# An early-fusion transformer block: the second pair's embedding moved into the prologue, and the negative maxima split on GpSimd

## The chip, the core and the metric

The kernel runs on one core of one Trainium2 chip. Its engines are TensorE (PE, with its weight loads PEld), VectorE (DVE), ScalarE (ACT), GpSimd (POOL) and SyncE (SP), each with its own instruction stream; they wait for each other on semaphores. The metric is the device time of one execution, in microseconds (us), as the median of several runs.

## The reference

Eight images go through one block, and everything is float32.

```python
def tokenise(x, W):                       # x: 8, C=64, T=128, V=64
    xp = pad(x, 8 steps of T at the end, mode='edge')
    patches = xp[:, :, idx, :]            # 16 patches of 16 steps, stride 8
    xf = rfft(patches, axis=steps, norm='ortho')      # 9 frequencies
    return concat([xf.real, xf.imag]) @ W.T           # 1024 tokens of 64
h = concat([tokenise(x, W), txt])         # 1056 tokens: 1024 + 32 of text
h = h + attention(layernorm(h))           # 4 heads of 16, softmax, projection
h = h + moe(layernorm(h))                 # 8 experts 64-128-64, gelu, top 2 of 8
```

## The kernel before

**Pairs and slots.** Two images make a pair, one on partitions 0 to 63 and one on 64 to 127; there are four pairs. The patches, the transform and the weight are folded into one matrix `tok_m`, so that a half of a pair's tokens (512) is embedded by eight *steps* accumulating in one PSUM bank; a step is two float32 matmuls, one for each image, which the trace shows as four passes (`embed`, L1205). Then follow centring, variances (L458), the inverse roots by Newton steps on VectorE (`newton_step`, L479), their spreading by matmul (L505) and the scaling to `xn` (L1105). The attention takes the eight images one after the other in eight *slots* (`run_phase1`, L364). A slot has three chunks of queries (384, 384, 288) of 33 *units* each: a unit computes scores for one head and one tile of 128 keys (L1196, bf16), ScalarE exponentiates them (L932), and eight units later, each fourth unit, four heads are multiplied with the values (L1174, float32). Three banks hold scores. The last part of the kernel, the experts, is not touched.

**Maxima.** The softmax subtracts each query's exact maximum. So the scores are also computed beforehand with queries on the partitions (`maxima`, L1217; a matmul of 512 columns, L1233) and reduced by VectorE out of three further banks (L1044): 73 entries a slot with the shifts, hosted some 41 units ahead, most of an image's first chunk beside the previous image. After a chunk's last maximum VectorE takes the negative maximum (`negm`, L1058), splits it in three bf16 parts by four small dependent operations (L1067 to L1074), TensorE transposes them (*shift*, L1255), VectorE copies the result (`m_part`, L1083) and SyncE stores it under the query stack by three DMAs (L795); the first scores of the chunk (L1192) wait for these. `max_order` (L74) writes the order out: the shift of a chunk stands behind the first two maxima of the next chunk.

**Queries and keys.** A projection (L1287) is split in three bf16 parts by ScalarE, VectorE and GpSimd (L941, L1089, L1092, L861), and DMAs interleave the parts into the stacks `qs` and `ks` (L752; for the first image ScalarE issues those of `ks`, L948). The first maxima wait for the stacks.

**What goes on beside the units** is set by lists of unit numbers at the head of the file (`AT_EMBED`, `AT_TOKENISE`, `AT_FINISH` and so on) and put in one order for all engines by `side_steps` (L305): each engine walks the same list and does its own part, in order. Slot 0 tokenises pair 1, slot 2 pair 2, slot 4 pair 3; its 16 embedding steps stand at every second unit, 34 to 48 and 50 to 64. Slots 2, 4 and 6 also finish a pair's attention (L1313), for which GpSimd normalises the heads (L867). All of these take turns in one PSUM bank, counted by `side_full` and `side_free`.

**The prologue** does the same for pair 0 without cover: x in eight transfers and edges, embedding, normalisation, projection, stacks, values (L1292, evacuated by ScalarE, L954 and L961), and then the 32 maxima and shifts that belong before slot 0. SyncE loads x of pair 1 behind the stacks, 14 of 21 transfers at once (`X_EARLY`) and the others beside slot 0 (`load_x`, L673). `xt` is one buffer of 17 blocks, so a pair can be loaded only when the one before it is embedded; a half reads its own eight blocks and the one after them.

The order of an image's maxima is written out like this:

```python
order += [(0, c, 0), (0, c, 1), (0, c - 1, None)] + [(0, c, i) for i in range(2, MAX_OF[c])]
```

## Time and profile before

| what | value |
|---|---|
| median of 3 runs | 852.92 us (852.79 to 853.16) |
| the profiled execution's own time | 856.51 us |
| its span, first to last instruction | 854.7 us |
| TensorE busy | 783.5 us, 92% of the span |
| VectorE busy | 542.5 us, 63% |
| ScalarE busy | 460.8 us, 54% |
| GpSimd busy | 131.6 us, 15% |
| mean granted clock of TensorE | 0.945 |
| slot 0 begins, slot 1 begins | 89.8 us, 182.3 us |

The profile is one execution. A matmul's end is modelled, so that a busy TensorE isn't necessarily at its peak. The granted clock is given as a share of 2.4 GHz: 1.00 is that level, 0.50 the other, 1.2 GHz. In a row of the timeline or of a group, `out<-in` names the tiles, `x4` the number of instructions, and what stands in brackets is the idle time before them and what ended it. The chain of waits is followed back from the last instruction, at each step to what released it.

### The profile page before, as it was taken

The numbers are of one execution on the slowest core, as the hardware profiler recorded it, in microseconds if no ns is written. First come the engines' busy times: TensorE is split into PE (matmuls) and PEld (weight loads), VectorE is DVE, ScalarE is ACT, GpSimd is POOL, SyncE is SP. The second block draws the span as 40 slices with busy tenths as digits, with TensorE's granted clock in tenths as the row PEclk, the third lists the DMA queues.
The fourth block names the chain that finished last, engine by engine and source line by source line (L and its number), as shares of the span: only waits on it lengthen the run. The fifth ranks groups of instructions, "written<-read, shape, count | busy, mean of one in ns | idle before, by whom it ended". The sixth has DMA issues, their size and how long they took to land.

```text
span 854.7 us, 14341 instructions
## 1 busy us (share of the span) xinstructions
PE 783.5 (92%) x5352; PEld 304.7 (36%) x5352; DVE 542.5 (63%) x1181; ACT 460.8 (54%) x1069; POOL 131.6 (15%) x148
## 2 busy tenths in 40 slices
PE   1858899999999999999998999999988899999995
PEld 1342222433342243334224333433334344545442
DVE  5037664688876468887646588778864174656642
ACT  1100454566674456667445466766755655564662
POOL 0010100012000001201000110010100055463664
PEclk9955699999999999999999699999999999999998
DMA  9319121016621001662100110120000736465571
GB/s 194 76 52 196 58 59 38 2 48 143 112 79 66 1 2 58 133 112 86 59 2 1 41 53 2 48 97 1 15 2 2 140 81 133 101 133 100 118 140 26
DMA packets 61933, 60.03 MB, mean 70 GB/s; under 512 B 23840, under 2 KB 54056, under 8 KB 61864
## 3 DMA queue, kind: packets, MB, share of 16 engines
q1 hardware_dynamic: 59264, 57.58, 30.7%
q10 hardware_dynamic: 2599, 1.54, 0.9%
q8 instruction: 42, 0.69, 0.3%
q14 instruction: 28, 0.22, 0.1%
HBM read 38.88 MB, written 2.57 MB: 48 GB/s over the span
## 4 chain that ended last, share of the span: by engine, by line
PE 75%; DVE 14%; ACT 3%; DMA 3%; issue 2%; SPq 1%; POOL 0%; ACTq 0%; POOLq 0%; DVEq 0%
PE bank L1174 14%; PE bank L1196 13%; PE bank L1233 11%; PE bank L1210 8%; PE bank L1345 6%; PE bank L1328 6%; DVE max_parts L1044 5%; PE bank L1287 3%; PE bank L1179 2%; PE bank L462 2%; PE bank L513 2%; DMA q_stack<-m_part 1%; PE bank L638 1%; DMA proj_in<-in_L_attn_w_proj 1%; ACT probs L932 1%
## 5 line engine op out<-in xcount | busy, mean ns | idle before, releaser
L1044 DVE TENSOR_REDUCE max_parts<-bank 128x1 f32<-128x512 f32 x512 | 329.4, 683 | 123.4 <-PE bank L1233 121.9
L932 ACT ACTIVATE probs<-bank 128x384 f32<-128x384 f32 (+1 forms) x768 | 311.0, 466 | 175.8 <-PE bank L1196 174.1
L1196 PE MATMUL bank<-q_stack,k_stack 99*128 99x384 bf16 (+1 forms) x768 | 225.6, 322 | 2.7 <-ACT probs L932 2.4
L1233 PE MATMUL bank<-k_stack,q_stack 96*128 96x512 bf16 x512 | 205.2, 404 | 4.4 <-DVE max_tail L1052 1.8
L1174 PE MATMUL bank<-probs,v_tiles 128*32 128x384 f32 (+1 forms) x1536 | 156.4, 480 | 2.2 <-ACT heads_out L917 2.1
L1196 PEld LDWEIGHTS bank<-q_stack,k_stack 99*128 99x128 bf16 x768 | 72.0, 99 | 189.3 <-ACT probs L932 139.6
L984 ACT ACTIVATE hid<-bank,biases 128x704 f32<-128x704 f32 x96 | 77.7, 844 | 57.9 <-PE bank L1345 57.6
L1131 DVE SCALAR_TENSOR_TENSOR prod<-bank,biases,cwb 128x352 f32<-128x352 f32 x96 | 55.3, 580 | 64.6 <-PE bank L1328 54.8
L881 POOL TENSOR_TENSOR acc<-acc,prod 128x352 f32<-128x352 f32 x84 | 78.2, 931 | 59.7 <-DVE prod L1131 55.7
L861 POOL TENSOR_TENSOR part<-qk_rest,part 128x352 bf16<-128x352 f32 x24 | 20.4, 850 | 361.6 <-DVE part L1092 361.6
L1233 PEld LDWEIGHTS bank<-k_stack,q_stack 96*128 96x128 bf16 x512 | 50.6, 99 | 54.9 <-DVE max_parts L1044 30.3
L1328 PE MATMUL bank<-hid,w_sb 128*64 128x352 f32 x384 | 68.9, 478 | 1.3 <-DVE prod L1131 1.3
L1210 PE MATMUL bank<-x,tok_m 128*64 128x512 f32 x256 | 68.2, 631 | 1.7 <-DVE tok_m L1026 1.1
L867 POOL TENSOR_TENSOR on<-heads_out,recip 128x352 f32<-128x352 f32 x24 | 21.9, 934 | 218.3 <-DMA recip<-recip_rows 218.3
L1174 PEld LDWEIGHTS bank<-probs,v_tiles 128*32 128x32 f32 x1536 | 30.8, 109 | 61.1 <-ACT probs L932 40.6
L1345 PE MATMUL bank<-xn,w_sb 64*128 64x352 f32 x192 | 35.6, 488 | 0.6 <-ACT hid L984 0.6
L1328 PEld LDWEIGHTS bank<-hid,w_sb 128*64 128x64 f32 x384 | 23.4, 137 | 34.8 <-issue 27.9
L1345 PE MATMUL bank<-xn_odd,w_sb 64*128 64x352 f32 x192 | 35.2, 483 | 0.6 <-ACT hid L984 0.6
L941 ACT ACTIVATE part<-bank 128x352 bf16<-128x352 f32 x24 | 11.1, 463 | 33.7 <-PE bank L1287 33.5
L925 ACT ACTIVATE probs_tail<-bank 128x384 f32<-128x384 f32 (+1 forms) x24 | 11.1, 462 | 33.7 <-PE bank L1192 33.7
L513 PE MATMUL bank<-ident_half,root_part 128*64 128x128 bf16 (+1 forms) x432 | 18.1, 231 | 10.4 <-DVE root_part L503 7.4
L1287 PE MATMUL bank<-xn,qkT 64*128 64x352 f32 x48 | 26.0, 637 | 1.0 <-DVE xn L1105 0.6
(146 smaller groups left out, 541.9 us busy)
## 6 DMA issues: line engine op xcount, KB each, us to landing
cwb<-gates_by_expert SPq DMA_DIRECT2D x24, 704.0 KB, 11.3
x<-in_x SPq DMA_DIRECT2D x48, 256.0 KB, 6.9
q_stack<-part SPq DMA_DIRECT2D x48, 132.0 KB, 2.4
k_stack<-part SPq DMA_DIRECT2D x42, 132.0 KB, 2.5
x<-in_x SPq DMA_DIRECT2D x4, 576.0 KB, 11.3
h_res<-h_new SPq DMA_DIRECT2D x4, 528.0 KB, 3.0
recip<-recip_rows SPq DMA_DIRECT2D x32, 66.0 KB, 2.5
h_all<-h_res SPq DMA_DIRECT2D x4, 528.0 KB, 3.0
```

What stands on the lines that cost most here:

```text
L881: nc.gpsimd.tensor_tensor(dst, h2_all[:, p, chunk[c]] if e == 0 else dst, prod[:, n % N_PROD, :], ALU.add).then_inc(summed, 1)
L932: nc.scalar.activation(probs[:, group % 3, h, 0:n], src, ACT.Exp, scale=SCALE).then_inc(exp_done, 1)
L984: nc.scalar.activation(hid[:, n % N_HID, :, :], psum[:, first:first + 2, 0:CH], ACT.Gelu, bias=b1_sb[:, e:e + 1]).then_inc(gelu_done, 1)
L1044: nc.vector.tensor_reduce(max_parts[:, c, H * j + h, i % 2:i % 2 + 1], src[:, :], AX.X, ALU.max)\
L1131: nc.vector.scalar_tensor_tensor(out=prod[:, n % N_PROD, :], in0=banks[4 + n % 2][:, 0:CH], scalar=b2_sb[:, e:e + 1], in1=cwb[p % 2][:, e, ...
L1174: last = nc.tensor.matmul(o_bank[32 * h:32 * h + 32, 0:n], v_tiles[par][:, kt, h, :], probs[:, group % 3, h, 0:n], start=(kt == 0), stop=F ...
L1196: last = nc.tensor.matmul(bank[:, 0:n], ks[par][0:ROWS + 3, h, P * kt:P * kt + P], qs[par][0:ROWS + 3, h, QC[qc]], start=True, stop=True)
L1210: last = nc.tensor.matmul(bank[D * bp:D * bp + D, :], tok_m[:, part, :], xt[bp][:, first:first + NPATCH // 2, t4, :], start=(part == 0), s ...
L1233: last = nc.tensor.matmul(bank[:, :], queries(h, j), ks[par][0:ROWS, h, HALF * (i % 2):HALF * (i % 2) + HALF], start=True, stop=True)
L1287: last = nc.tensor.matmul(bank[:, 0:CH], qkT[rows, :], xn[rows, chunk[i]], start=True, stop=True)
L1328: last = nc.tensor.matmul(banks[4 + n % 2][D * bp:D * bp + D, 0:CH], w2_sb[:, m % E, :], hid[:, n % N_HID, bp, :], start=True, stop=True)
L1345: last = nc.tensor.matmul(banks[2 * (n % 2) + bp][:, 0:CH], w1_sb[rows, e, :], xn2[p % 2][rows, chunk[c]], start=True, stop=True)
```

## The change

**Loading.** The second pair's x is loaded in halves by eight larger transfers and four edges: the first half when pair 0's first half is embedded, the second when its second half is, both issued by SyncE ahead of the copy of `h_res`; the text follows that. `X_EARLY` and slot 0's loads are gone. **Embedding.** The sixteen steps of pair 1 and the two evacuations into `h_new` leave slot 0: six steps come behind the values of image 0, ten among the prologue's maxima (`AHEAD_BESIDE`: behind entries 3, 6, 9, ... of the 32). Slot 0 keeps the rest of the tokenising (`settle`). In slots 2 and 4 the steps stand in pairs, two at each fourth unit. **Values.** Image 0's are evacuated by VectorE. **Negative maxima.** The four splitting operations go from VectorE to GpSimd, for all 24 chunks, and the shift comes behind three maxima of the next chunk rather than two. The diff, cut to its core:

```diff
@@ -59,7 +59,7 @@
...
 AT_STACK = [1, 3]
-AT_EMBED = [list(range(34, 49, 2)), list(range(50, 65, 2))]
+AT_EMBED = [[34, 34, 38, 38, 42, 42, 46, 46], [50, 50, 54, 54, 58, 58, 62, 62]]
@@ -67,15 +67,19 @@
...
 X_DMAS = 4 * (X_CUTS + 1) + 1
-X_EARLY = 14
-AT_LOAD = {"first": [2 + 3 * k for k in range(X_DMAS - X_EARLY)], "load": [30 + 3 * k for k in range(X_DMAS)]}
+X_SECOND = 13
+AT_LOAD = [30 + 3 * k for k in range(X_DMAS)]
+AHEAD = 2
+AHEAD_BEFORE, AHEAD_BESIDE = 6, [3, 6, 9, 12, 15, 18, 21, 24, 29, 30]
...
+SHIFT_AFTER = 3
...
-    order = [(0, 0, 0), (0, 0, 1), (-1, NCH - 1, None)] + [(0, 0, i) for i in range(2, MAX_OF[0])]
+    order = [(0, 0, i) for i in range(SHIFT_AFTER)] + [(-1, NCH - 1, None)] + [(0, 0, i) for i in range(SHIFT_AFTER, MAX_OF[0])]
     for c in range(1, NCH):
-        order += [(0, c, 0), (0, c, 1), (0, c - 1, None)] + [(0, c, i) for i in range(2, MAX_OF[c])]
+        order += [(0, c, i) for i in range(SHIFT_AFTER)] + [(0, c - 1, None)] + [(0, c, i) for i in range(SHIFT_AFTER, MAX_OF[c])]
@@ -210,6 +214,7 @@
...
         neg_max = sem("neg_max")
+        neg_found = sem("neg_found")
@@ -284,8 +289,9 @@
...
         g_values0 = USES["tokenise"] + USES["project"]
-        g_slot0 = g_values0 + USES["values"]
-        g_slot1 = g_slot0 + 2 * USES["project"] + USES["tokenise"]
+        g_ahead = g_values0 + USES["values"]
+        g_slot0 = g_ahead + AHEAD
+        g_slot1 = g_slot0 + 2 * USES["project"] + USES["tokenise"] - AHEAD
@@ -316,10 +322,8 @@
...
                 order.append(("normalise", AT_NORMALISE.index(u), b - 1, 1 - par, q, g))
-            if "load" in stages and u in AT_LOAD["load"]:
-                order.append(("load", AT_LOAD["load"].index(u), None, None, q + 2, g))
-            if "first" in stages and u in AT_LOAD["first"]:
-                order.append(("load", X_EARLY + AT_LOAD["first"].index(u), None, None, 1, g))
+            if "load" in stages and u in AT_LOAD:
+                order.append(("load", AT_LOAD.index(u), None, None, q + 2, g))
@@ -327,18 +331,22 @@
...
                     ("tokenise", "tokenise", AT_TOKENISE, None, None, q + 2),
+                    ("settle", "tokenise", AT_TOKENISE, None, None, q + 2),
...
                 if name in stages:
+                    done = AHEAD if name == "settle" else 0
+                    g = g - done
+                    if name == "tokenise":
+                        for i in range(2):
+                            for part, at_part in enumerate(AT_EMBED[i][:-1]):
+                                if u == at_part:
+                                    order.append(("embed", (i, part), None, None, pair, g))
...
                         order.append(("vary", AT_VARY.index(u), None, None, pair, g))
-                    if u in at:
+                    if u in at and at.index(u) >= done:
                         order.append((stage, at.index(u), t, tpar, pair, g))
-                    if stage == "tokenise":
-                        for i in range(2):
-                            if u in AT_EMBED[i][:-1]:
-                                order.append(("embed", (i, AT_EMBED[i].index(u)), None, None, pair, g))
-                        if u in AT_ROOT:
-                            order.append(("root", 1 + AT_ROOT.index(u), None, None, pair, g))
+                    if stage == "tokenise" and u in AT_ROOT:
+                        order.append(("root", 1 + AT_ROOT.index(u), None, None, pair, g))
@@ -357,7 +365,7 @@
         NEXT = ("following", "normalise")
-        BESIDE = {0: ("following", "first", "tokenise", "project"), "odd": NEXT + ("load", "project"),
+        BESIDE = {0: ("following", "first", "settle", "project"), "odd": NEXT + ("load", "project"),
@@ -391,9 +399,15 @@
...
                 side("values", i, 0, None, 0, g_values0)
-            for u in range(MAX_PLACE[0], 0):
-                for _, c, i, n in hosted(u, True, False):
-                    side("maxima" if i is not None else "shift", (c, i, n), 0, 0, None, None)
+            ahead = [("embed" if part < 7 else "tokenise", (half, part) if part < 7 else half, None, None, 1, g_ahead)
+                     for half in range(AHEAD) for part in range(8)]
+            for step in ahead[:AHEAD_BEFORE]:
+                side(*step)
+            early = [found for u in range(MAX_PLACE[0], 0) for found in hosted(u, True, False)]
+            for k, (_, c, i, n) in enumerate(early):
+                side("maxima" if i is not None else "shift", (c, i, n), 0, 0, None, None)
+                if k in AHEAD_BESIDE:
+                    side(*ahead[AHEAD_BEFORE + AHEAD_BESIDE.index(k)])
@@ -442,8 +456,8 @@
...
             if isinstance(t, int) and t == 0:
-                at = n if n < 2 else n - 1
-                return at, n % 3, at - 1 if n in (3, 4) else at - 2
+                at = n if n < SHIFT_AFTER else n - 1
+                return at, n % 3, at - 1 if n in (SHIFT_AFTER + 1, SHIFT_AFTER + 2) else at - 2
@@ -688,19 +702,22 @@
...
-        def load_first_x(eng):
...
-            for half, (first, n) in enumerate(((0, NPATCH // 2 + 1), (NPATCH // 2 + 1, NPATCH // 2 - 1))):
+        def load_half_x(eng, pair, half, blocks, done):
...
+            first, n = blocks
+            for bp in range(2):
+                for th in range(2):
+                    eng.dma_start(xt[bp][C * th:C * th + C, first:first + n, :, :],
+                                  x[2 * pair + bp].rearrange("c (j h t) v -> h c j t v", h=2, t=4)[th, :, first:first + n])\
+                       .then_inc(done, 16)
+            if half == 1:
...
                     for th in range(2):
-                        eng.dma_start(xt[bp][C * th:C * th + C, first:first + n, :, :],
-                                      x[bp].rearrange("c (j h t) v -> h c j t v", h=2, t=4)[th, :, first:first + n])\
-                           .then_inc(x_half[half], 16)
-            for bp in range(2):
-                for th in range(2):
-                    eng.dma_start(xt[bp][C * th:C * th + C, NPATCH, :, :],
-                                  x[bp][:, T - 1:T, :].broadcast_to([C, 4, V])).then_inc(x_half[1], 16)
-            eng.dma_start(text_in[:, :, :], txt[0:2].rearrange("b t d -> t b d")).then_inc(x_half[1], 16)
+                        eng.dma_start(xt[bp][C * th:C * th + C, NPATCH, :, :],
+                                      x[2 * pair + bp][:, T - 1:T, :].broadcast_to([C, 4, V])).then_inc(done, 16)
...
+        def load_text(eng, pair, done):
+            eng.dma_start(text_in[:, :, :], txt[2 * pair:2 * pair + 2].rearrange("b t d -> t b d")).then_inc(done, 16)
@@ -743,7 +760,9 @@
...
             def _(sp):
-                load_first_x(sp)
+                load_half_x(sp, 0, 0, (0, NPATCH // 2 + 1), x_half[0])
+                load_half_x(sp, 0, 1, (NPATCH // 2 + 1, NPATCH // 2 - 1), x_half[1])
+                load_text(sp, 0, x_half[1])
@@ -781,10 +800,6 @@
...
                         stack_parts(t, par, range(3, 6))
-                        if isinstance(t, int) and t == 0:
-                            sp.wait_ge(side_full, 3)
-                            for k in range(X_EARLY):
-                                load_x(sp, 1, k)
@@ -800,9 +815,14 @@
...
                         load_ffn(sp)
-                    elif stage == "tokenise" and isinstance(pair, int) and pair == 0 and i == 3:
+                    elif stage == "tokenise" and pair == 0 and i < 2:
...
+                        sp.wait_ge(side_full, i + 1)
+                        load_half_x(sp, 1, i, (NPATCH // 2 * i, NPATCH // 2), x_loaded)
+                    elif stage == "tokenise" and pair == 0 and i == 3:
...
                         sp.dma_start(h_res[:, :], h_new[:, :]).then_inc(h_copied, 16)
+                        load_text(sp, 1, x_loaded)
@@ -860,6 +880,21 @@
...
                                                 ALU.subtract).then_inc(part3_done, 1)
+                    elif stage == "maxima" and i[1] == MAX_OF[i[0]] - 1:
...
+                        c = i[0]
+                        k = NCH * t + c
+                        kinds = slice(0, 1) if c < NCH - 1 else slice(1, 3)
+                        pool.wait_ge(neg_found, k + 1)
+                        nc.gpsimd.tensor_copy(neg_part[:, kinds, :, 0, :], negm[:, kinds, :, :]).then_inc(neg_step, 1)
+                        pool.wait_ge(neg_step, 3 * k + 1)
+                        nc.gpsimd.tensor_tensor(neg_rest[:, kinds, :, :], negm[:, kinds, :, :],
+                                                neg_part[:, kinds, :, 0, :], ALU.subtract).then_inc(neg_step, 1)
+                        pool.wait_ge(neg_step, 3 * k + 2)
+                        nc.gpsimd.tensor_copy(neg_part[:, kinds, :, 1, :], neg_rest[:, kinds, :, :]).then_inc(neg_step, 1)
+                        pool.wait_ge(neg_step, 3 * k + 3)
+                        nc.gpsimd.tensor_tensor(neg_part[:, kinds, :, 2, :], neg_rest[:, kinds, :, :],
+                                                neg_part[:, kinds, :, 1, :], ALU.subtract).then_inc(neg_max, 1)
@@ -946,7 +981,7 @@
...
                             act.dma_start(ks[par][n:ROWS:len(PARTS), :, 0:L], qk_part[k][D:P, :]).then_inc(stacked, 16)
-                    elif stage == "values":
+                    elif stage == "values" and t > 0:
@@ -1053,7 +1088,6 @@
...
                             dve.wait_ge(max_done, at + 1)
-                            step = 4 * (NCH * t + c)
@@ -1062,17 +1096,7 @@
...
                                                                    AX.X, ALU.max, negate=True)
-                            last.then_inc(neg_step, 1)
-                            dve.wait_ge(neg_step, step + 1)
-                            nc.vector.tensor_copy(neg_part[:, kinds, :, 0, :], negm[:, kinds, :, :]).then_inc(neg_step, 1)
-                            dve.wait_ge(neg_step, step + 2)
-                            nc.vector.tensor_tensor(neg_rest[:, kinds, :, :], negm[:, kinds, :, :],
-                                                    neg_part[:, kinds, :, 0, :], ALU.subtract).then_inc(neg_step, 1)
-                            dve.wait_ge(neg_step, step + 3)
-                            nc.vector.tensor_copy(neg_part[:, kinds, :, 1, :], neg_rest[:, kinds, :, :]).then_inc(neg_step, 1)
-                            dve.wait_ge(neg_step, step + 4)
-                            nc.vector.tensor_tensor(neg_part[:, kinds, :, 2, :], neg_rest[:, kinds, :, :],
-                                                    neg_part[:, kinds, :, 1, :], ALU.subtract).then_inc(neg_max, 1)
+                            last.then_inc(neg_found, 1)
@@ -1090,6 +1114,21 @@
...
                         nc.vector.tensor_copy(qk_part[1][:, chunk[i]], qk_rest[:, chunk[i]]).then_inc(part2_done, 1)
+                    elif stage == "values" and t == 0:
+                        bank = full(dve, i, g)
+                        if i < 2:
+                            tiles = slice(KT // 2 * i, KT // 2 * i + KT // 2)
+                            for bp in range(2):
+                                last = nc.vector.tensor_copy(
+                                    v_tiles[bp][:, tiles, :, 0:DH],
+                                    bank[:, :].rearrange("p (k a h d) -> p a k h d", a=2, h=H, d=DH)[:, bp])
+                        else:
+                            for h in range(H):
+                                rows = slice(32 * h, 32 * h + 32)
+                                for bp in range(2):
+                                    last = nc.vector.tensor_copy(v_tail[bp][rows, 32 * h:32 * h + DH],
+                                                                 bank[rows, DH * bp:DH * bp + DH])
+                        last.then_inc(side_free, 1)
@@ -1268,7 +1307,7 @@
...
                             elif half == 0:
-                                pe.wait_ge(x_loaded, 16 * X_DMAS * pair)
+                                pe.wait_ge(x_loaded, 16 * (X_SECOND + X_DMAS * (pair - 1)))
...
```

## Rows read from the trace of the kernel before

**Rows 1.** the page: the span and the granted clock in 40 slices (tenths)

```profile
span 854.7 us, 14341 instructions
...
PEclk9955699999999999999999699999999999999998
```

**Rows 2.** stretches, slots 0, 1, 2, 4: busy per engine, clock, DMA share, GB/s

```profile
89.76:182.34 92.58, 90.55 (x575) 30.16 (x575) 57.78 (x125) 47.62 (x115) 4.86 (x6) 0.91 0.13 36
...
182.34:242.59 60.25, 58.35 (x425) 20.12 (x425) 49.65 (x99) 41.28 (x105) 5.50 (x7) 1.00 0.52 108
...
242.59:330.99 88.40, 86.74 (x607) 30.80 (x607) 57.11 (x123) 48.27 (x125) 5.03 (x6) 0.98 0.10 35
...
390.83:484.82 93.99, 91.14 (x606) 32.05 (x606) 57.22 (x123) 48.35 (x125) 5.26 (x6) 0.93 0.10 33
```

**Rows 3.** the chain that ended last, prologue: start us, us, what

```profile
62.13 5.83 DMA k_stack<-part
...
87.93 1.79 DMA q_stack<-m_part
...
89.76 0.51 PE bank L1192 x4
```

**Rows 4.** stretches of the prologue and of the start of slot 0

```profile
0.00:22.00 22.00, 3.51 (x44) 2.94 (x44) 12.92 (x25) 2.18 (x6) 0.20 (x4) 1.00 1.05 194
...
68.00:89.80 21.80, 17.86 (x47) 3.50 (x47) 19.65 (x37) 0.07 (x2) 0.00 (x0) 0.50 0.89 154
...
89.80:102.50 12.70, 12.70 (x36) 3.75 (x37) 7.60 (x14) 5.61 (x12) 2.55 (x3) 0.52 0.09 28
```

**Rows 5.** timeline of TensorE, first pair's embedding: windows from 20 and from 27.69

```profile
22.33 16.25 PE L1210 MATMUL bank<-x,tok_m 128*64 128x512 f32 x64 [1.12 <-DVE tok_m L1026]
...
27.69 10.89 PE L1210 MATMUL bank<-x,tok_m 128*64 128x512 f32 x50
```

**Rows 6.** timeline, values in the prologue and a VectorE copy in slot 0

```profile
57.11 2.07 PE L1292 MATMUL bank<-vT,xn 128*128 128x128 f32 x8 [1.11 <-DVE qk_rest L1089]
...
63.13 0.66 ACT L954 ACTIVATE v_tiles<-bank 128x256 f32<-128x256 f32 x2 [6.63 <-issue]
...
67.07 1.00 ACT L961 ACTIVATE v_tail<-bank 32x16 f32<-32x16 f32 x8 [0.46 <-PE bank L1296]
...
152.57 0.69 DVE L1096 COPY h_new<-bank 128x512 f32<-128x512 f32 x1
```

**Rows 7.** DMA issues of x: KB each, median us to landing

```profile
x<-in_x SPq DMA_DIRECT2D x48, 256.0 KB, 6.9
```

**Rows 8.** the chain that ended last, slot 0

```profile
105.45 0.33 PE bank L1196 x2
...
117.64 1.01 PE bank L1210 x4
...
121.93 0.27 PE bank L1196
```

**Rows 9.** timeline of SyncE, the early transfers of x

```profile
63.09 12.86 SPq L679 DMA_DIRECT2D x<-in_x  x14
```

**Rows 10.** groups of instructions on GpSimd: busy, mean ns, idle before

```profile
L861 POOL TENSOR_TENSOR part<-qk_rest,part 128x352 bf16<-128x352 f32 x24 | 20.4, 850 | 361.6 <-DVE part L1092 361.6
...
L1412 POOL MEMSET const-float32-1.0<- 128x1 f32 x1 | 0.1, 98 | 0.0
```

**Rows 11.** the chain that ended last, slot 1's second chunk

```profile
197.17 1.27 DVE max_parts L1044 x2
...
200.26 1.78 DMA q_stack<-m_part
```

**Rows 12.** a stretch of slot 4

```profile
464.00:470.00 6.00, 4.11 (x69) 2.29 (x67) 5.47 (x19) 2.21 (x7) 0.00 (x0) 1.00 0.00 0
```

**Rows 13.** the chain that ended last, slot 4

```profile
467.72 0.18 DVE neg_part L1067
...
468.49 0.48 DVE xn L1105
```

## The prediction

> **What bounds the kernel now.** I read the page first, for the span and the clock row [rows 1]: TensorE is granted its upper level (2.4 GHz) nearly everywhere, and the lower one (1.2 GHz) in two places, slices 3 and 4 (43 to 85 us, from the table of stretches on to 102) and one slice near 480. Then I cut the attention into its slots [rows 2]. TensorE is busy 90.6 of 92.6 us in slot 0, 86.7 of 88.4 in slot 2 and 58.4 of 60.3 in slot 1, so work taken from it there shortens the slot; slots 0, 2 and 4 are longer than the odd ones because a pair is tokenised beside them. Last, the chain of waits of the prologue [rows 3]: the stacks land at 68.0 (62.13 + 5.83), first maxima run to the shift whose DMA starts at 87.93, and slot 0 begins at 89.76. In these 21.8 us VectorE is busy 19.7, 0.61 us for each of some 31 maxima, TensorE at the lower clock 17.9; in the first 12.7 us of slot 0 TensorE is busy throughout, still at 0.52 of its clock [rows 4].
>
> The profiled execution took 856.5 us (span 854.7 and 1.8 around it), 3.6 above the median of 852.9. I work out a difference within the profile and take it from the median.
>
> **A. The 16 embedding steps of pair 1, before slot 0.** What precedes them: values 0 leaves TensorE at 59.2 [rows 6]; in the kernel before, ScalarE issues six stack DMAs first and evacuates only at 63.13. On VectorE, which is idle there, each half of the values is two 256-column copies; from the 512-column copy of 0.69 us [rows 6] I take 0.75 for both (ScalarE: 0.66). The eight small copies were 1.00 on ScalarE; I take 1.1. Then: 59.2 + 0.75 + 2.07 + 0.75 + 0.34 + 1.1 = 64.3 us, from which embedding may start (0.3 estimated for the tail's small matmuls).
>
> Is x there? A pair is 16 transfers of 256 KB [rows 7] and four edge rows a quarter of that, 4.35 MB. Half of it may be issued when the first half of pair 0 is embedded (31.7 by the slow and fast passes below), the rest at 38.6 when the second is (the end of the 16.25 us row, [rows 5]). At the 194 GB/s of the first 22 us [rows 4] that is 11 us each, so all lands near 54; at the 154 of the maxima stretch, near 60. SyncE now issues fourteen in 12.86 us, 0.92 each [rows 8]; the second eight keep it until 46, with the copy of h_res and the text behind them, and it is free again before the stacks. The copy of h_res so lands some 7 us later; its reader is the second pair's first evacuation, beyond 70. Cost nothing, and if x were late by t, t.
>
> Six steps (24 matmul passes) come ahead of the maxima. In pair 0's embedding 50 passes took 10.89 us, 0.218 each, 0.87 a step; the whole 64 took 16.25 [rows 5], which fits 12 passes at twice that. So I take 12 slow passes and 12 fast: 5.2 + 2.6 = 7.8, ending at 72.1. The ends: 5.2 if the clock is up already (69.5), 10.5 if it doesn't rise (74.8). First maxima at 68.0 become 72.1: **+4.1** (+1.5 to +6.8). The stacks can only land earlier, x no longer sharing their queue, and hide behind the six steps.
>
> Ten steps lie among the maxima. At the upper clock an isolated step is 1.01 us and the score matmul after it 0.27 where a pair takes 0.33, so 0.105 more [rows 9]: 1.11 us. With three maxima at 0.22 (512 columns, as a pass of the embedding) that is 1.77 against VectorE's 1.83. They fit, barely, with two finished banks in hand; the last two lie behind the shift, where TensorE waits for its DMA. Their evacuation (0.69) is VectorE's and also behind the shift. I take **+0.3**.
>
> **B. Slot 0.** It loses 16 isolated steps: 16 x 1.11 = **-17.8**. And it starts at the upper clock: of 12.6 slow us TensorE would need 6.3, but VectorE's 7.6 [rows 4] and gaps of 0.8 then bound, so 8.4: **-4.2**. The sum, 70.6, stands against slot 1's 60.3 [rows 2] with some 10 to 12 us of the remaining tokenising and second projection on top, so no floor is broken. The slower end, clock down again at the slot's start, is 0 in place of -4.2.
>
> **C. Steps in pairs, slots 2 and 4.** The second step of a pair is free of the switch: 1.11 - 0.87 = 0.24, eight times a slot, two slots: **-3.9**. A block of 1.9 us lets ScalarE run dry, but over slot 2 it is busy 0.49 of each unit's 0.89 [rows 2]; if it does hurt, the other end is +2.
>
> **D. Negative maxima on GpSimd, the shift one maximum later.** VectorE loses four operations a chunk, in slot 4 0.77 us from the first (467.72) to the next tile's work (468.49) [rows 13]. GpSimd shows none so small: above, 0.85 us for 352 columns; below, 0.10 for a one-column memset [rows 10]. By the line between them 12 columns are 0.13; with semaphores I take 0.22, four are 0.9, near the lower row because the operand is. For two-input elementwise work the Trainium skill (GPSIMD Engine Reference, 4.1 Engine selection) calls GpSimd the wrong engine, about twice slower than VectorE; with the 0.18 of such an operation now doubled for two or all of the four, the chain would be 1.1 to 1.4. No run here shows it yet.
>
> Three maxima (1.83 us) now cover this chain instead of two, and VectorE reaches the shift's copy no later: the two maxima at 197.17 start 0.8 after they could [rows 11]. So slots 1, 3, 5 and 7, whose second chunk waits for the shift's DMA (until 202.04 in slot 1 [rows 11]), gain 0.8 each, **-3.2**. The 19 other hand-overs cost nothing of themselves, hidden by scores and maxima. In slots 0, 2 and 4 the chain of roots and maxima holds TensorE (busy 4.1 of 6.0 us, [rows 12]) and the four operations stand right in it [rows 13]: 3 x 0.77 = **-2.3**. GpSimd's normalising now queues behind the split; in slot 6 the finishing matmul, a unit after the shift, then waits, an estimated **+0.6**, and slot 7's last shift, with no maxima to cover it, **+0.3**.
>
> **Sum**: 4.1 + 0.3 - 17.8 - 4.2 - 3.9 - 3.2 - 2.3 + 0.9 = -26.1; 852.9 - 26.1 = **826.8 us**.
>
> **Rivals.**
> **The clock stays down through the prologue.** For it: TensorE was fully busy for 12.7 us at the lower level before it rose [rows 4]. Against: by its passes, the first embedding rose within its first 5 us [rows 5], and this is the same work. Six steps then end at 74.8 (+6.8); a group of three maxima and a step costs 3 x 0.43 + 1.9 = 3.2 against 1.83, eight times (+11), the last two +2; no clock is won back in slot 0. With C and D (-8.5): 19.8 - 17.8 - 8.5 = -6.5: 846.4. The Trainium skill (TensorE: Matmul & The Clock Gate, Part 1) has the lower level as the default that activity lifts; the embedding row agrees, the start of slot 0 less plainly. 10%.
> **GpSimd is dear (the slower case).** At 0.85 an operation the chain is 3.4 us, the copy of the shift 1.8 later than now, and TensorE stands in order before the shift with scores queued behind it. With 24 hand-overs, all exposed, +43; the 14 outside the prologue and the tokenising slots alone, +25. Against A to C's -21.5 that is 856 to 875, say 864. With all exposed it decides from about 0.62 us an operation (24 x (1.8 - 4 x 0.23) = 21). For it: only the 0.85 row has this engine's arithmetic. Against: 352 columns aren't 12. 4%.
> **The change moves the work but gains nothing**: x late by 20 us or more, or the ten steps starve VectorE. Against: the 10 us in hand above. Near 852. 2%.
> **Clock dips.** The slice near 480 is a dip behind that starved stretch; slot 4 is 5.6 longer than slot 2 for it [rows 2]. With D the stretch is fuller and the dip may go: 821.2, 20%. Or it comes at slot 0's start as well: 831.0, 15%. Both lie in the range.
>
> **Numbers.** Forecast as it stands, 49%. The range, 815.5 to 839, holds it, both dips, and the ends of A to D short of the low-clock prologue. A measurement can tell 0.2% (1.7 us) from no change. Faster 0.94: all but the dear GpSimd, the empty case and a remainder; slower 0.04, same 0.02.
>
> **What would show it.** In the changed profile: x landed before 60; 24 embedding passes between 64 and 72, then maxima at 0.61 us spacing; full granted clock by 72 and at slot 0's start, near 94.2; slot 0 near 70 long; slots 2 and 4 shorter by 2 to 3; GpSimd's four operations about 0.2 us each, no wait of the shift matmul for them over 0.5. It is wrong if the maxima run slower than 0.7 us apart, if slot 0 starts after 98, or if the shift matmuls wait for GpSimd by a microsecond each.

## The result and the profile after

| | before | changed |
|---|---|---|
| median of 4 runs | 853.04 us | 832.83 us |
| range | 852.79 to 854.58 | 832.56 to 835.82 |
| profiled execution, its span | 856.51, 854.7 | 832.62, 830.8 |
| mean granted clock in it | 0.945 | 0.966 |

The change is faster: the ratio is 0.9742, with a 95% interval of 0.9688 to 0.9795; 20.2 us less, where 26.1 less were forecast (826.8; the range was 815.5 to 839). The page of the changed kernel, its span and its clock row, against [rows 1]:

```profile
span 830.8 us, 14333 instructions
...
PEclk9968899999999999999999999999999999999998
```

A part of slices 3 and 4 is still at the lower level (44.5 to 51.3 and 54.7 to 68.3 us), a part of slice 5 is at it too, and the dip near 480 us isn't there. By slots (slots 0, 1, 2 and 4 of the changed kernel, columns as in [rows 2]):

```profile
93.08:167.57 74.49, 72.18 (x510) 27.88 (x510) 54.40 (x112) 45.61 (x114) 7.38 (x18) 0.91 0.12 34
167.57:226.91 59.34, 57.89 (x425) 20.12 (x424) 47.41 (x87) 41.09 (x105) 7.99 (x19) 1.00 0.53 110
226.91:314.47 87.56, 84.99 (x606) 32.09 (x606) 55.13 (x111) 47.49 (x125) 7.50 (x18) 0.98 0.11 36
373.81:461.34 87.53, 84.95 (x606) 32.10 (x606) 55.14 (x111) 47.50 (x125) 7.49 (x18) 0.98 0.11 36
```

Slot 0 begins 3.3 us later and is 74.5 us long in place of 92.6; slot 1 is 0.9 shorter, slot 2 0.8. Slot 4 is 6.5 shorter, of which 5.6 are the dip that the profiled execution of before happened to have there: it had been that much longer than slot 2, at the same work. From slot 7 on nothing changed (249.0 to the end, 248.9 before). Over the two profiles that makes -23.9, without the dip -18.3; the medians say -20.2. The profiled execution of before was 3.5 above its median, so the truth lies between the two sums.

The prologue, from the timeline of the changed kernel (start us, duration, engine, line; in brackets the idle time before and what ended it), against [rows 3], [rows 5] and [rows 6]:

```profile
41.53 7.09 SPq L716 DMA_DIRECT2D x<-in_x  x4
...
57.68 0.75 DVE L1122 COPY v_tiles<-bank 128x256 f32<-128x256 f32 x2 [1.47 <-PE bank L1331]
...
61.81 1.07 DVE L1129 COPY v_tail<-bank 32x16 f32<-32x16 f32 x8 [0.46 <-PE bank L1335]
63.02 7.99 PE L1249 MATMUL bank<-x,tok_m 128*64 128x512 f32 x24 [1.28 <-DVE v_tail L1129]
70.95 0.82 PE L1272 MATMUL bank<-k_stack,q_stack 96*128 96x512 bf16 x3
...
93.08 0.35 PE L1231 MATMUL bank<-q_stack,k_stack 99*32 99x384 bf16 x4 [1.07 <-DMA q_stack<-m_part]
```

VectorE's evacuations are 0.75 and 1.07, forecast 0.75 and 1.1; the 24 passes ahead of the maxima take 7.99, forecast 7.8; the first maxima come at 71.0, forecast 72.1, and slot 0 starts at 93.1, forecast 94.2. The 1.1 us is TensorE's projection, which met a higher clock. SyncE issued x and its edges until 48.6, forecast 46, and the first stack transfer at 57.25 was not delayed; the embedding waited for VectorE's evacuation and not for x. What the forecast did not take as its case is seen a little further on, in stretches of 2 us (columns as in [rows 4]):

```profile
88.00:90.00 2.00, 1.19 (x6) 0.39 (x6) 2.00 (x5) 0.00 (x0) 0.52 (x3) 1.00 0.00 0
90.00:92.00 2.00, 2.00 (x8) 0.39 (x6) 1.09 (x3) 0.00 (x0) 0.00 (x0) 1.00 0.01 3
92.00:94.00 2.00, 0.93 (x7) 0.49 (x7) 1.24 (x3) 0.49 (x1) 0.00 (x0) 1.00 0.01 2
94.00:96.00 2.00, 1.76 (x7) 0.66 (x6) 1.38 (x4) 1.23 (x3) 0.00 (x0) 0.91 0.00 0
96.00:98.00 2.00, 2.00 (x5) 0.58 (x5) 1.45 (x3) 0.77 (x2) 0.85 (x1) 0.50 0.00 0
98.00:100.00 2.00, 2.00 (x5) 0.50 (x2) 1.79 (x4) 0.64 (x2) 0.85 (x1) 0.50 0.00 0
100.00:102.00 2.00, 2.00 (x7) 0.75 (x7) 1.17 (x3) 1.50 (x4) 0.22 (x1) 0.50 0.00 0
102.00:104.00 2.00, 2.00 (x11) 0.34 (x9) 1.61 (x3) 0.79 (x2) 0.63 (x1) 0.50 0.05 15
104.00:106.00 2.00, 2.00 (x9) 0.74 (x6) 0.69 (x1) 0.90 (x3) 0.00 (x0) 0.53 0.65 209
```

TensorE is at 2.4 GHz from 68 us through the maxima, idle for about 0.8 us before the shift and 1.07 us for the shift's DMA, and at 95.7 it falls to the lower level and stays there till 105.9 (the last row's 0.53). Slot 0's first chunk takes 26.15 us, little less than the 26.83 of before.

### The profile page after: what moved, and what is told of

Read it like the earlier page. It is cut to its first block, busy times and chain, and to the rows that moved or that the text cites. A ratio compares the mean times of both kernels' runs of the same rounds, so it can differ in the third digit from the quotient of the medians.

```text
span 830.8 us, 14333 instructions
## 1 busy us (share of the span) xinstructions
PE 762.5 (92%) x5352; PEld 306.7 (37%) x5352; DVE 529.5 (64%) x1097; ACT 455.2 (55%) x1057; POOL 151.7 (18%) x244
## 4 chain that ended last, share of the span: by engine, by line
PE 78%; DVE 10%; ACT 4%; issue 2%; DMA 2%; POOL 1%; ACTq 1%; SPq 1%; POOLq 0%; DVEq 0%
PE bank L1213 16%; PE bank L1235 14%; PE bank L1272 12%; PE bank L1249 7%; PE bank L1367 6%; PE bank L1384 6%; DVE max_parts L1079 3%; PE bank L1326 2%; PE bank L1218 2%; PE bank L527 2%; PE bank L476 2%; DVE max_tail L1087 1%; DMA q_stack<-m_part 1%; ACT probs L967 1%; PE bank L1331 1%
## 5 line engine op out<-in xcount | busy, mean ns | idle before, releaser
L967 ACT ACTIVATE probs<-bank 128x384 f32<-128x384 f32 (+1 forms) x768 | 307.5, 466 | 155.6 <-PE bank L1235 154.1
L1272 PE MATMUL bank<-k_stack,q_stack 96*128 96x512 bf16 x512 | 196.3, 389 | 4.7 <-DVE max_tail L1087 3.2
L889 POOL CAST neg_part<-negm 128x12 bf16<-128x12 f32 (+1 forms) x24 | 4.7, 198 | 428.7 <-DVE negm L1092 330.2
L1249 PE MATMUL bank<-x,tok_m 128*64 128x512 f32 x256 | 66.5, 649 | 3.0 <-DVE v_tail L1129 1.3
L1249 PEld LDWEIGHTS bank<-x,tok_m 128*64 128x64 f32 x256 | 17.5, 147 | 35.5 <-issue 34.0
L1004 ACT ACTIVATE h_new<-bank 128x512 f32<-128x512 f32 (+1 forms) x8 | 3.2, 397 | 44.1 <-PE bank L1249 37.5
```

What stands on the lines that cost most here:

```text
L967: nc.scalar.activation(probs[:, group % 3, h, 0:n], src, ACT.Exp, scale=SCALE).then_inc(exp_done, 1)
L1249: last = nc.tensor.matmul(bank[D * bp:D * bp + D, :], tok_m[:, part, :], xt[bp][:, first:first + NPATCH // 2, t4, :], start=(part == 0), s ...
L1272: last = nc.tensor.matmul(bank[:, :], queries(h, j), ks[par][0:ROWS, h, HALF * (i % 2):HALF * (i % 2) + HALF], start=True, stop=True)
```

## The experiments

Because the clock falls at other places in other executions, I compare mostly the lengths of chunks, from one chunk's first scores (`L1192` in the kernel before) to the next's; where the clock is up and GpSimd splits the maxima they repeat within 0.1 us, and where VectorE splits them they differ by up to 0.4 (22.00 and 22.36 in slots 2 and 4 of `e5_early_only`). The changed kernel, e1 to e4, e5 to e8 and e9 to e12 are four groups, each measured beside the kernel before, whose median was 853.0, 857.1, 859.0 and 855.6: ratios are to be compared, not medians across groups. The start of slot 0 also moves with the clock in the prologue: three kernels with the same prologue (changed, e1, e6) have it between 92.86 and 94.42. "Slot 2" gives its three chunks; "odd" is slot 3's first chunk.

| kernel | median (range) us | ratio, 95% interval | slot 0 starts | its first chunk | slot 0 | odd | slot 2 |
|---|---|---|---|---|---|---|---|
| before | 853.0 | 1 | 89.76 | 26.83 | 92.58 | 19.34 | 21.99, 38.23, 28.18 |
| changed | 832.8 (832.6 to 835.8) | 0.974 (0.969 to 0.980) | 93.08 | 26.15 | 74.49 | 19.11 | 22.34, 37.37, 27.85 |
| e1_singles | 835.9 (830.7 to 838.4) | 0.974 (0.969 to 0.979) | 92.86 | 26.06 | 74.43 | 19.15 | 22.34, 38.34, 27.41 |
| e2_split_vector | 839.4 (833.3 to 840.4) | 0.977 (0.972 to 0.982) | 92.76 | 22.62 | 71.38 | 19.83 | 21.77, 37.37, 28.39 |
| e3_fill | 830.3 (829.4 to 831.2) | 0.968 (0.964 to 0.972) | 91.69 | 21.82 | 70.15 | 19.12 | 22.33, 37.38, 27.84 |
| e4_shift_two | 831.3 (831.2 to 835.4) | 0.970 (0.966 to 0.974) | 92.69 | 21.42 | 69.80 | 18.77 | 22.33, 37.48, 27.78 |
| e5_early_only | 842.1 (835.3 to 844.2) | 0.980 (0.974 to 0.985) | 92.95 | 21.85 | 70.67 | 19.23 | 21.99, 38.23, 28.18 |
| e6_pairs_moved | 830.2 (828.0 to 834.2) | 0.967 (0.962 to 0.972) | 94.42 | 26.16 | 74.51 | 19.13 | 22.34, 36.41, 27.43 |
| e7_values_scalar | 836.6 (831.7 to 839.8) | 0.975 (0.969 to 0.981) | 97.19 | 26.03 | 74.40 | 19.13 | 22.33, 37.38, 27.81 |
| e8_best | 825.6 (824.8 to 826.3) | 0.962 (0.958 to 0.966) | 90.10 | 21.82 | 70.17 | 19.12 | 22.33, 36.41, 27.42 |
| e9_no_fill | 829.2 (825.2 to 832.0) | 0.969 (0.964 to 0.973) | 89.85 | 21.81 | 69.76 | 19.10 | 22.34, 36.40, 27.81 |
| e10_fill_last | 826.5 (825.5 to 827.1) | 0.966 (0.962 to 0.970) | 89.50 | 21.81 | 70.39 | 19.12 | 22.34, 36.41, 27.84 |
| e11_normalise_first | 822.6 (820.5 to 828.9) | 0.962 (0.958 to 0.967) | 90.39 | 21.82 | 70.19 | 19.12 | 21.57, 36.41, 27.42 |
| e12_four_ahead | 822.5 (821.4 to 824.1) | 0.961 (0.957 to 0.966) | 89.77 | 21.81 | 69.76 | 19.13 | 21.57, 36.41, 28.04 |

### The early embedding alone

```diff
 (the changed kernel, with the split on VectorE, SHIFT_AFTER = 2 and single steps)
-AT_EMBED = [[34, 34, 38, 38, 42, 42, 46, 46], [50, 50, 54, 54, 58, 58, 62, 62]]
+AT_EMBED = [list(range(34, 49, 2)), list(range(50, 65, 2))]
-SHIFT_AFTER = 3
+SHIFT_AFTER = 2
```

> The kernel before with the early loading, the early embedding and the values on VectorE alone: the split is on VectorE, the shift behind two maxima, the steps of slots 2 and 4 single. The forecast's A and B: slot 0 starts at 94.2 and is 70.6 long, 835 in all; with its clock dip at the start 839. My theory after the first runs: slot 0 starts near 93 and is 71 to 75 long with the clock, slots 2 and 4 88.4, odd slots 59.8 to 60.2 as in the kernel before; 837 to 840, so that the split and the pairs together are worth 5 to 7 of the 20. Rival: the early embedding gives everything, 833.

Measured: ratio 0.980, so about four fifths of the gain, though the intervals of the two ratios overlap. In its profiled execution slot 0 starts at 92.95 and is 70.67 long, all but 3.4 us at the upper clock (forecast 94.2 and 70.6); slot 2 is that of before, slot 4 is 89.1 long. Both slots as stretches of that profile:

```profile
92.95:163.62 70.67, 68.01 (x512) 26.65 (x512) 55.88 (x125) 45.02 (x114) 4.87 (x6) 0.98 0.12 36
224.39:312.79 88.40, 85.34 (x605) 30.31 (x605) 57.17 (x123) 48.27 (x125) 5.01 (x6) 1.00 0.11 35
```

The median is over my 837 to 840, and its six executions lie in two groups, 835.3 and 835.4 with a mean clock of 0.973 and four from 840.7 to 844.2 with 0.957 to 0.960. The four are 5 to 9 us longer at their lower mean clock; where in them it fell isn't recorded. The 70.67 agrees with the forecast partly by luck. The first chunk, which holds no embedding step, went from 26.83 to 21.85, so the clock was worth 5.0 rather than 4.2; the second chunk, which held all sixteen steps, went from 37.02 to 20.63, so a step was worth 1.02 rather than 1.11.

### The clock at slot 0's start

```diff
+FILL = {27: 4, 31: 5}
                 if k in AHEAD_BESIDE:
                     side(*ahead[AHEAD_BEFORE + AHEAD_BESIDE.index(k)])
+                if k in FILL:
+                    side("fill", FILL[k], None, None, None, None)
...
+                    if stage == "fill":
+                        for _ in range(i):
+                            nc.tensor.matmul(score_bank[0][:, :], qs[0][0:ROWS, 0, 0:P], ks[0][0:ROWS, 0, 0:HALF],
+                                             start=True, stop=True)
+                        return
```

> The changed kernel plus nine idle matmuls of 512 bf16 columns on TensorE that nothing reads: four behind entry 27 of the prologue's maxima (before the shift), five behind the last (while the shift's DMA is under way). They lie in two gaps of about 1 us. Theory: the clock falls at 95.8 because TensorE was busy only 6 of the 8 us before; held up, slot 0 loses no 10 us at the lower clock and gets back the forecast's 4.2: 828.6, granted clock 1.00 between 94 and 106. Rival: the fall has another cause (the projections, which follow), and it comes all the same: 832.8 to 833.5.

The idle matmuls write a score bank that the first real scores overwrite; nothing is left out of the computation. Measured: the first chunk is 21.82 in place of 26.15, 4.3 less (the forecast's price of this clock was 4.2), all four executions between 829.4 and 831.2. But in the profiles of e2, e4 and e5, which have no such matmuls, the first chunk was short too (in e2 the clock fell earlier, from 89.8 to 93.2, and rose again), so one profile proves little. The question was put again on a better kernel (`e8_best`, below), with all of the idle matmuls, with none, and with the last five alone, in six executions each:

```diff
 (the kernel of e8_best)
-FILL = {27: 4, 31: 5}
+FILL = {}            (e9_no_fill)
+FILL = {31: 5}       (e10_fill_last)
```

> The kernel of e8_best without its nine idle matmuls (moved pairs and three banks for the values kept). Theory: the gaps of about 1 us at the end of the prologue let the clock fall in the first chunk of slot 0 in some or most executions, which costs 4.3: the median is 2 to 4.5 above e8_best's 825.6 (827.6 to 830) and its executions spread by 3 us or more, where e8_best's lay within 1.5. Rival: what steadied e8_best were the three banks (other times against the clock's own), and the idle matmuls do nothing: 825.6 and as narrow.

> The kernel of e8_best with only the five idle matmuls behind the last of the prologue's maxima, where TensorE waits for the shift's DMA. Theory: one of the two gaps filled is half the remedy; if the later gap decides, 825.6 as e8_best; if both count, between, with some executions at 829. Rival (idle matmuls do nothing): as e9_no_fill.

Measured, with none: 825.2, 825.9, 827.0 and 831.4, 831.9, 832.0, the first three at a mean clock of 0.970 to 0.973, the others at 0.962 or 0.963. With the last five: all six between 825.5 and 827.1. With nine: all six between 824.8 and 826.3. Over all profiles with idle matmuls the first chunk was 21.8 in five of five; without them (the kernel before left aside) it was 26.0 to 26.2 in four of eight, and with e2's short fall the clock fell near slot 0's start in five of eight. The stretches of `e8_best` where the gaps had been:

```profile
88.00:90.00 2.00, 2.00 (x10) 0.51 (x6) 1.67 (x3) 0.00 (x0) 0.00 (x0) 1.00 0.02 5
90.00:92.00 2.00, 2.00 (x11) 0.80 (x11) 0.72 (x2) 0.90 (x3) 0.00 (x0) 1.00 0.03 8
92.00:94.00 2.00, 1.76 (x8) 0.61 (x6) 1.88 (x4) 1.27 (x5) 0.85 (x1) 1.00 0.00 0
```

TensorE is busy 2.00, 2.00 and 1.76 us of each 2, where the changed kernel had 0.93 and 1.19 in places. So the idle time at the end of the prologue most likely lets the clock fall, in about half of the executions, and with five matmuls in the wait for the shift's DMA no execution of six was long. The three long executions of `e9_no_fill` have no profile: that they fell at this place is only inferred from their length, 5 to 6 us more, and their clock. The inference isn't safe by itself, since `e11_normalise_first` has the idle matmuls and yet took 828.9 at a mean clock of 0.962 in its profiled execution, for a fall in slot 7. The Trainium skill (TensorE: Matmul & The Clock Gate, Part 1) has the lower level as the default that activity lifts: these runs agree so far that with added activity the upper level stayed at slot 0's start in five profiles of five, a first chunk of 21.8, and without it fell in some, 26.1.

### The values on VectorE, and in three banks

```diff
-                    elif stage == "values" and t > 0:
+                    elif stage == "values":
 (and VectorE's branch for t == 0 taken out)
```

> The changed kernel with image 0's values evacuated by ScalarE again, behind its six stack DMAs. Theory: the first evacuation waits for the end of these issues, near 62, the embedding starts at 67 rather than 63, the first maxima at 75 rather than 71: slot 0 starts 4 to 4.5 later, near 97.3, 837 in all. Rival: the six steps run slow or fast by the clock whatever their start, and a later start meets a higher clock: 1 to 2 us later only.

The 24 passes then start 4.3 later than at 63.02, and slot 0 at 97.19 rather than 93.08, 4.1 later; they took as long (the first row below, from the timeline):

```profile
67.30 7.79 PE L1234 MATMUL bank<-x,tok_m 128*64 128x512 f32 x24 [1.21 <-ACT v_tail L996]
```

So the move of the evacuation, which the change's title doesn't mention, is worth 4.1 us at the start of slot 0. The ratios of the whole time, 0.975 and 0.974, don't show it across the groups; against `e6_pairs_moved` of the same group it is 836.6 to 830.2, of which the moved pairs are 1.9. `e8_best` takes it on by giving the three groups a bank each, and puts the idle matmuls and the moved pairs with it:

```diff
-            return isinstance(g, int) and g < g_values0
+            return isinstance(g, int) and g <= g_values0
-            return in_prologue(g) and g + i in (1, 2, 4, 5, 8, 9, 11, 12)
+            return in_prologue(g) and g + i in (1, 2, 4, 5, 8, 9, 11, 12, 14, 15)
```

> The changed kernel with three things together: the nine idle matmuls in the gaps at the end of the prologue, the moved pairs, and the three groups of image 0's values in three PSUM banks rather than one, so that TensorE doesn't wait for VectorE between them. Theory: embedding starts 1.2 us earlier, near 61.8, slot 0 keeps its clock (4.3) and slots 2 and 4 lose 1 to 1.9 each: 832.8 - 1.2 - 3.5 - 3 = 825. Rival: the clock, not these, decides, and only the moved pairs show: 830.

Measured: 825.6, and the embedding starts at 61.07, 1.95 earlier. From the first matmul of the values to the first of the embedding it is 5.7 us in place of 7.5, which is what the three banks give; the passes took 1.0 less by the clock:

```profile
61.07 6.95 PE L1253 MATMUL bank<-x,tok_m 128*64 128x512 f32 x24 [1.65 <-DVE v_tail L1133]
```

### The steps in pairs

```diff
-AT_EMBED = [[34, 34, 38, 38, 42, 42, 46, 46], [50, 50, 54, 54, 58, 58, 62, 62]]
+AT_EMBED = [list(range(34, 49, 2)), list(range(50, 65, 2))]                      (e1_singles)
+AT_EMBED = [[34, 34, 40, 40, 43, 43, 48, 48], [50, 50, 54, 54, 58, 58, 62, 62]]  (e6_pairs_moved)
```

> The changed kernel with one thing undone: the embedding steps of slots 2 and 4 stand singly at every second unit again. Changed kernel: 832.8. The forecast's theory (a pair saves one switch of 0.24 us, sixteen pairs, nothing lost) expects 3.9 more, 836.7, with slots 2 and 4 longer by 1.9 each. My theory after the two traces: the switches are saved, but the pairs at units 38 and 46 uncover a wait for the evacuation of the heads and one for the last maxima, about 1 us each, so a pair slot gains only some 0.4 to 0.9: 833.6 to 834.6. A rival (pairs gain nothing at all, slots 2 and 4 gained from the split alone) expects 832.8 or less.

> The changed kernel with the first half's pairs in slots 2 and 4 at units 34, 40, 43 and 48 in place of 34, 38, 42 and 46. Theory: behind the pair at 38 TensorE waits 1.0 us for ScalarE's evacuation of the heads, behind that at 46 1.1 us for the last maxima; at 40 and 48 the same pairs cover these waits. The second chunk of slots 2 and 4, 37.37 in the changed kernel, becomes 35.5 to 36.4, the time 2 to 3.5 less than the changed kernel's. Rival: the waits are VectorE's and ScalarE's load, not the pair's place, and move along: 37.4 and no gain.

Measured in the second chunk of slots 2 and 4, where the steps lie: single 38.34, in pairs 37.37, in moved pairs 36.41. So pairs gained 0.97 a slot, half of the forecast's 1.95, and pairs in better places 1.93. The chain of waits of the changed kernel in slot 2 shows the other half:

```profile
256.42 1.87 PE bank L1249 x8
258.29 0.28 PE bank L1235
258.57 0.02 issue
258.59 0.49 ACT probs L967
259.08 0.39 ACT heads_out L952
259.47 0.14 issue
259.61 0.85 PE bank L1213 x8
...
267.60 0.53 DVE max_tail L1087
268.12 0.01 issue
268.13 0.54 DVE max_tail L1087
268.66 0.14 issue
268.80 0.38 PE bank L1272
```

The pair at unit 38 (256.42) stands ahead of the scores of unit 39, behind whose exponentials ScalarE evacuates the heads; the product with the values that needs the bank comes 1.3 us after these scores. At 268.8 the next image's first maximum waits for the last ones of this image. At units 40 and 48 the same pair of 1.87 lies inside these waits. TensorE's waits bear it out: in the changed kernel's second chunk it waits 0.3 us for the heads and 0.5 for the last maximum and is idle 1.04 in all; both waits are gone, and 0.29 is left, with the moved pairs of `e6_pairs_moved` and with the single steps of `e1_singles`. For the whole time `e1_singles` against the changed kernel decides nothing (0.9735 and 0.9742): single executions of it went from 830.7 to 838.4 with the clock.

### The split on GpSimd and the later shift

```diff
 e2_split_vector: the four operations back behind negm on VectorE, SHIFT_AFTER = 3
 e4_shift_two: the four operations on GpSimd,
-SHIFT_AFTER = 3
+SHIFT_AFTER = 2
```

> The changed kernel with the four splitting operations back on VectorE and the shift still behind three maxima. The forecast's theory: VectorE's 0.77 us a chunk stands on the path in the second chunk of slots 1, 3, 5 and 7 and in the roots' stretch of slots 0, 2 and 4, so 5 more: 838. Rival: the shift's place in TensorE's order, not VectorE's time, sets the second chunk; then only the roots' stretches lose, 1.5 to 2.3 in all, 834.5 to 835, and the wait before slot 1's second chunk stays at 0.55.

> The changed kernel with the shift behind two maxima as before, the split still on GpSimd. Theory: GpSimd's chain takes 1.05 us from negm, two maxima 1.25, so they just cover it; the copy of the shift comes 0.6 us earlier against the chunk's start and the waits of 0.55 for the shift's DMA in the second chunk of slots 1, 3, 5 and 7 vanish: 2 us less, 830.8. Rival: with two maxima TensorE reaches the shift before GpSimd is done and stands 0.3 to 0.5 us in some twelve hand-overs: 4 us more, 837.

GpSimd's operations in the changed kernel (the tile `neg_part`: min/median/max in ns):

```profile
L889 POOL CAST neg_part<-negm x24: 194/194/206, 87.6 to 612.2; 128x12 bf16<-128x12 f32 x16, 128x24 bf16<-128x24 f32 x8
L891 POOL TENSOR_TENSOR neg_rest<-negm,neg_part x24: 213/214/240, 87.9 to 612.4; 128x12 f32<-128x12 f32 x16, 128x24 f32<-128x24 f32 x8
```

0.19 and 0.21 us, forecast 0.22 with the wait between; the starts are 0.27 apart (87.63, 87.90, 88.18, 88.45), so the chain is 1.05, forecast 0.9. That rival is out.

Where the time was forecast, in the first chunk of an odd slot, the four kernels read: before 19.34, GpSimd with the shift behind two 18.77, GpSimd behind three 19.11, VectorE behind three 19.83. So VectorE's 0.77 does stand on this path in good part (0.72 between the two with the shift behind three, 0.57 between the two behind two), but the later shift gives 0.34 of it back. The chain of the changed kernel there:

```profile
329.01 0.23 PE bank L1272
...
329.88 0.27 DVE m_part L1107
...
331.00 0.73 SPq L810
331.73 0.04 issue
331.78 1.76 DMA q_stack<-m_part
333.54 0.04 issue
333.58 0.35 PE bank L1231 x4
```

It is no longer the split that ends last. The third maximum comes at 329.01, when its place in TensorE's order comes; VectorE reduces it from 329.27 on and can copy the shift only then, at 329.88. From there copy, issue and DMA take 3.7 us, and TensorE stands 0.56 for them. With the shift behind two maxima, in turn, it meets GpSimd's chain in the third chunks, 17.85 against 17.39 (the timeline of TensorE of `e4_shift_two`):

```profile
216.33 0.22 PE L1294 MATMUL bank<-ident_half,neg_part 128*36 128x128 bf16 x1 [0.45 <-POOL neg_part L896]
```

So the two places are worth the same within 0.3 us a slot, except in slot 6, which is 0.56 longer with the shift behind two. In the roots' stretch of slots 2 and 4 the forecast's 0.77 is there: third chunk 28.18 before and in `e5_early_only`, 27.41 in `e1_singles` (27.8 where the clock dips in it).

And the first chunks of slots 2, 4 and 6 became longer, 22.34 against 21.99. The cause stands in the timeline of slot 2 (the first two rows are of the changed kernel's GpSimd and TensorE):

```profile
243.24 2.71 POOL L902 TENSOR_TENSOR on<-heads_out,recip 128x352 f32<-128x352 f32 x3
244.31 0.81 PE L1352 MATMUL bank<-on,projT 128*64 128x352 f32 x4 [0.56 <-POOL on L902]
```

The finishing matmul waits 0.56 for the normalising behind the split, in all three slots and not in slot 6 alone. One number removes it:

```diff
-AT_NORMALISE = [24, 26, 28]
+AT_NORMALISE = [21, 26, 28]
```

> The kernel of e8_best with GpSimd's first normalising operation a unit before the split of the second chunk's negative maxima in its order, rather than two units behind it. Theory: TensorE's first finishing matmul of slots 2, 4 and 6 waits 0.56 us for the normalising queued behind the split; without it their first chunks, 22.33, become 21.8 to 21.9: 1.5 less, 824.1. Rival: the wait is made up before the next chunk, or the normalising now delays the split and with it the shift: no gain.

Measured: these chunks are 21.57 to 21.59, 0.75 less each and so 2.3 in all. In the whole time it isn't seen against `e8_best` (ratio 0.962 for both); within its own group it has 822.6 where `e10_fill_last`, with four idle matmuls fewer, has 826.5. Its executions range from 820.5 to 828.9 (the profiled one, clock 0.83 in slot 7's second chunk).

### A version that beats both

```diff
 (the kernel of e11_normalise_first)
-AHEAD_BEFORE, AHEAD_BESIDE = 6, [3, 6, 9, 12, 15, 18, 21, 24, 29, 30]
+AHEAD_BEFORE, AHEAD_BESIDE = 4, [1, 3, 6, 8, 11, 13, 16, 18, 21, 24, 29, 30]
```

> The kernel of e11_normalise_first with four embedding steps ahead of the prologue's maxima and twelve among them. Theory: the first maxima come 1.9 us earlier; TensorE's 2.5 maxima and a step, 1.66, are then more than VectorE's 1.52, which gives back 10 times 0.14 and some gaps: slot 0 starts 0 to 0.7 earlier, near 89.7. Rival: the buffers of three banks don't cover a step so often, VectorE starves: slot 0 starts 1 to 2 later.

Measured: slot 0 starts at 89.77, 0.6 before that of `e11_normalise_first`, with sixteen steps done before it and at the very time of the kernel before. That the order gives this 0.6 is likely but not shown: `e11_normalise_first` had the same clock in the prologue to within 0.3 us, but `e10_fill_last`, also with six steps ahead, started at 89.50 with a clock that had risen earlier. The ratio is 0.961 (0.957 to 0.966) against the changed kernel's 0.974, about 11 us; from `e11_normalise_first` (822.6, it 822.5) it can't be told in the whole time.

## Why the prediction was right and wrong

**A, the prologue (+4.4): right.** +3.3. The evacuations, the 24 passes and the maxima were within 0.2 us of the forecast; the projection ran faster (2.04 us, before 3.89). Two slips in the working didn't matter. The row of 16.25 us, redone with 0.218 a pass, holds 10 to 11 slow passes and not 12; and the isolated step and score matmuls are in [rows 8], SyncE's fourteen transfers in [rows 9], not the other way round. The maxima did stay VectorE's with a step among each three of them: 22.1 us from the first to slot 0, before 21.8. x was there in time.

**B, slot 0 (-22.0): right in its mechanism, wrong in one term.** 18.1 was measured, with slot 0's share of D in it. The step that failed is "it starts at the upper clock ... -4.2": I let the clock follow from the dense prologue and gave its fall at slot 0's start 15%. It fell there in four of eight profiles without idle matmuls, the changed kernel's among them. The length with the clock up was right, 70.6 forecast and 70.67 in `e5_early_only`, but by two errors that cancel: the clock was worth 5.0 and not 4.2, the steps 16.4 and not 17.8, and 0.6 came in the third chunk. What the fall costs the changed kernel, 4.3 in `e3_fill`, was near the 4.2. I had the two waits in view (I put the last two steps behind the shift) but didn't ask what they do to the clock.

**C, pairs (-3.9): mis-sized by half.** "If it does hurt" was the right doubt in the wrong place. ScalarE's mean load doesn't decide; the evacuation of the heads and the last maxima are waits with a reader close behind, and a block of 1.87 us adds to them or covers them according to the unit where it stands. 1.9 measured for the two slots, 3.9 with the pairs moved.

**D, the split (-4.6): about -3.** By the clean chunks of `e5_early_only` and `e1_singles`, slots 1 to 6 together are 2.7 shorter (1.4, 0.3, 0.3, 0.3 by slot 2, 0.4 and -0.1), and slot 0's third chunk, already counted in B, 0.8 (28.18 in `e5_early_only`, 27.42 in `e9_no_fill`). Of slot 1's 1.4, 1.0 is there because in `e5_early_only` two of VectorE's two-input splitting operations took 0.81 and 0.65 us, in place of 0.17, while GpSimd normalised (177.4 to 179.1 us); in the kernel before one took 0.65. On GpSimd the split stands ahead of the normalising and doesn't meet it. The roots' -0.77 each held. The -0.8 for each odd slot failed at "VectorE reaches the shift's copy no later": so it does, but the third maximum then comes late in TensorE's order, and 0.04 to 0.23 was left in slots 3, 5 and 7. The +0.6 for the normalising was the right mechanism and came in three slots instead of one; `e11_normalise_first` prices it at 0.75 each. The +0.3 for slot 7's last shift came as forecast: TensorE waits 2.37 us for it, before 2.06; of these the split is 1.3, before 1.0.

**The rivals.** The low clock through the prologue didn't come: it rose within the 24 passes, as by the rows of pair 0. The dear GpSimd didn't come either: its operations took 0.19 and 0.21 us, where 0.62 would have been needed. The dip that the forecast put at 831.0 is the case that happened, and 832.8 is 1.8 above it. The dip of slot 4 isn't in the profile of `e5_early_only`, which has the same work there; with one profile of the kernel before, whether it is a matter of the execution is likely but not shown.

With the measured parts the sum is +3.3 - 18.1 - 1.9 - 2.7 = -19.4, against -20.2 by the medians.

**Left open.** That the clock of slot 0's start falls for the two gaps rests on 18 executions of three kernels and 13 profiles; no long execution of `e9_no_fill` was profiled. Whether slot 4's dip has the same cause as slot 0's, and what sets the clock in slot 7 (its second chunk was 27.3 to 31.2 in these profiles), wasn't tried. Filling the second gap was enough; whether filling the first alone would be was not tried.

## What to carry over

Work moved into an idle stretch of TensorE is worth its full duration on the path that it leaves, and that can be summed from rows (here to 1.4 us in 17.8); but look at each gap of a microsecond that is left before a dense stretch, since it may cost several through the clock, and a few idle matmuls into a bank that is rewritten anyway are cheap insurance. Before work is gathered in larger blocks, list the hand-overs with a fixed distance (an evacuation, a last reduction) and put the blocks inside these waits. When an engine's share of a hand-over is taken away, ask what is next on it: here the order on TensorE, and the work queued behind on the engine that took the share over.

## What was not expected of the hardware

The same program had executions 5 to 6 us apart, the longer ones at a lower mean clock (825.2 to 827.0 and 831.4 to 832.0 in `e9_no_fill`), and the kernel before went from 850.3 us at a mean clock of 0.957 to 871.0 at 0.929 over the 29 executions beside the experiments, though its first four lay within 1.8. In the changed kernel the clock was down from 95.7 to 105.9, although TensorE was busy throughout in the stretches from 96 to 106. Four dependent operations on GpSimd of 12 columns start 0.27 apart, VectorE's 0.20. And a VectorE operation of that size with two inputs, 0.17 by itself, took up to 0.81 while GpSimd worked on 352 columns.
